# Centring the next image in four batches, one on VectorE and three on GpSimd, with the statistics and the products at other places

## The reference

```
x = x + DCT2(gn(x))                    # gn: per image and channel, (x - mean)/sqrt(var + eps)
y = gn(x)
for k in range(6):                     # Euler steps, dt = 1/6
    h = relu(gn(y)*g1 + b1);  h = conv3x3([t_k, h]) + c1
    h = relu(gn(h)*g2 + b2);  h = conv3x3([t_k, h]) + c2
    y = y + dt*(gn(h)*g3 + b3)
x = x + y
```

## Time and profile before

| | us |
|---|---|
| median of 3 runs | 3807.86 (3799.22 to 3810.55) |
| the profiled execution, its own time | 3808.01 |
| its span in the profile | 3806.2 |
| TensorE busy | 3070.4 (81%) |
| VectorE busy | 2698.6 (71%) |
| ScalarE busy | 2497.2 (66%) |
| GpSimd busy | 1026.3 (27%) |
| mean granted TensorE clock | 0.916 of full speed |

### The profile page before, as it was taken

One profiled execution on the slowest core, in us unless ns is written; L12 is line 12 of the kernel. 1 busy time (PEld: TensorE's weight loads), 2 busy tenths in 40 slices (PEclk: granted clock), 3 DMA queues, 4 the chain that ended last, 5 costly groups with the idle time before them and its releaser, 6 DMA issues.

```text
span 3806.2 us, 147663 instructions
## 1 busy us (share of the span) xinstructions
PE 3070.4 (81%) x61716; PEld 2552.5 (67%) x61716; DVE 2698.6 (71%) x6177; ACT 2497.2 (66%) x3867; POOL 1026.3 (27%) x1405
## 2 busy tenths in 40 slices
PE   3588888888878888788887888888888887888884
PEld 3576767667666666666676766766766666777773
DVE  7577777676767667666776677767776777768783
ACT  0466678566776567756676665866668666687774
POOL 4034312333133331333313333133321334111111
PEclk8799999899999899989998998989999999999997
DMA  3300023112131230312303213032131311321113
GB/s 81 77 20 19 20 53 88 44 53 69 29 88 47 65 69 15 88 54 78 62 3 96 78 45 61 16 91 70 45 61 39 93 45 45 62 69 47 54 45 103
DMA packets 368816, 217.55 MB, mean 57 GB/s; under 512 B 353152, under 2 KB 353520, under 8 KB 366064
## 3 DMA queue, kind: packets, MB, share of 16 engines
q1 hardware_dynamic: 368112, 207.63, 21.4%
HBM read 104.85 MB, written 77.07 MB: 48 GB/s over the span
## 4 chain that ended last, share of the span: by engine, by line
DVE 20%; issue 18%; PE 17%; POOL 17%; ACT 16%; DMA 7%; SPq 3%; DVEq 1%; POOLq 0%; ACTq 0%
POOL xn L556 12%; PE cps L1435 11%; ACT z L659 5%; DMA xs<-in_x_dram 5%; ACT z L689 4%; DVE bnt L1111 3%; PE dps L1543 3%; SPq L438 2%; POOL m L546 2%; DVE hb L1081 2%; DVE y L1085 2%; DVE bn L1130 2%; ACT unread_z L679 2%; DVE ha L1081 1%; DVE bni L1122 1%
## 5 line engine op out<-in xcount | busy, mean ns | idle before, releaser
L1435 PE MATMUL cps<-ha,w 64*64 64x392 f16 (+1 forms) x27648 | 1441.7, 353 | 97.6 <-issue 41.0
L659 ACT ACTIVATE z<-cps,bias_now 128x784 f32<-128x784 f32 (+2 forms) x1056 | 764.2, 740 | 839.1 <-PE cps L1435 833.4
L1435 PE MATMUL cps<-hb,w 64*64 64x392 f16 x27648 | 1274.0, 333 | 33.3 <-POOL hb L523 11.4
L1435 PEld LDWEIGHTS cps<-ha,w 64*64 64x64 f16 x27648 | 1081.8, 112 | 316.8 <-issue 139.3
L1435 PEld LDWEIGHTS cps<-hb,w 64*64 64x64 f16 x27648 | 1075.9, 107 | 134.9 <-issue 47.9
L503 POOL TENSOR_TENSOR small<-small,half 128x1 f32<-128x1 f32 x304 | 168.2, 553 | 1657.3 <-DVE small L1012 1242.1
L1111 DVE BATCH_NORM_STATS2 bnt<-z 128x6 f32<-128x392 f32 (+1 forms) x768 | 388.3, 551 | 238.3 <-ACT z L659 237.8
L1081 DVE TENSOR_TENSOR ha<-z,ha 128x784 f16<-128x784 f32 x384 | 381.4, 993 | 96.0 <-ACT z L689 92.2
L556 POOL TENSOR_SCALAR xn<-xs,m 112x112 f32<-112x112 f32 x448 | 438.6, 993 | 6.0 <-POOL m L551 6.0
L1081 DVE TENSOR_TENSOR hb<-z,hb 128x784 f16<-128x784 f32 x384 | 374.4, 975 | 84.7 <-ACT z L689 77.1
L689 ACT ACTIVATE z<-z,small 128x784 f32<-128x784 f32 x384 | 396.3, 1032 | 0.0
(11 more groups left out here) (161 smaller groups left out, 2679.3 us busy)
## 6 DMA issues: line engine op xcount, KB each, us to landing
xa<-x_dram SPq DMA_DIRECT2D x128, 196.0 KB, 5.0
y<-xa SPq DMA_DIRECT2D x16, 1568.0 KB, 7.5
y_dram<-y SPq DMA_DIRECT2D x128, 196.0 KB, 4.7
xs<-in_x_dram SPq DMA_DIRECT2D x31, 784.0 KB, 8.6
x_dram<-x1s SPq DMA_DIRECT2D x30, 784.0 KB, 5.3
fin<-y_dram SPq DMA_DIRECT2D x30, 784.0 KB, 8.1
fin<-x_dram SPq DMA_DIRECT2D x28, 784.0 KB, 8.5
out_dram<-fin SPq DMA_DIRECT2D x28, 784.0 KB, 3.3
```

The costliest lines, as they stand in the source:

```text
L659: return nc.scalar.activation(dst, src, ACT.Identity, bias=bias_now[parts, conv:conv + 1], **more)
L1435: return pe.matmul(dst, w[hin * 64:(hin + 1) * 64, kx, a, wl, :], src[:, :, 0:NA], start=(what == "X" and n == 0), stop=(what == "Y" and n ...
```

## The change

`normalise_half` is cut in two. `half_bias` (GpSimd) makes the product of mean and scale and stands right behind `half_rsqrt`. The 16 channels become four batches of four: batch 0 is a new `normalise_first` on VectorE, with a semaphore of its own, just ahead of the update of slot 0; batches 1 and 2 stay where all 16 were on GpSimd, batch 3 goes behind slot 1's powers. TensorE waits for each batch alone. On VectorE the statistics of the next half image are spread anew: four channels now stand between `pre_of(Z1, 0)` and `post_of(Z1, 0)`, together with the wait for the arrival of `xs`; then three, three, three, and three inside `post`. `half_post` goes from behind `products_of(1, 2)` to behind `split_for(2, 1)`, `products_of(1, 1)` behind it, and `products_of(1, 3)` ahead of `split_for(2, 3)`. In step FIVE the seven `start_stats` of slot 1 come from the end of FOUR, and `pre_of` and `post_of` of (IZ, 1) come later. On TensorE the statistics products move by some rounds.

```diff
--- before.py
+++ after.py
@@ -260,6 +260,7 @@
         s_xnb = sem("s_xnb")
         s_nb = sem("s_nb")
         xn_done = sem("xn_done")
+        xn_first = sem("xn_first")
         t_done = sem("t_done")
         ts_done = sem("ts_done")
         xp_done = sem("xp_done")
@@ -545,18 +546,21 @@
                 pool.wait_ge(s_m0, NHALF_STEPS * (n + 1))
                 nc.gpsimd.tensor_tensor(m[:, 4, 0:CQ], m[:, 3, CQ:2 * CQ], half[0:H, :], ALU.pow).then_inc(pow0, 1)
 
-            def normalise_half(n):
+            def half_bias(n):
 
                 pool.wait_ge(pow0, n + 1)
                 nc.gpsimd.tensor_tensor(m0[:, 6, CQ:2 * CQ], m0[:, 6, 0:CQ], m0[:, 4, 0:CQ], ALU.mult
                                         ).then_inc(s_nb, 1)
                 pool.wait_ge(s_nb, n - HALVES + 1)
+
+            def normalise(n, b):
+
                 pool.sem_inc(pool_gate, 1)
-                for c in range(CQ):
+                for c in range(4 * b, 4 * b + 4):
                     last = nc.gpsimd.tensor_scalar(xn[:, c, :], xs[:, c, :], m0[:, 4, c:c + 1],
                                                    m0[:, 6, CQ + c:CQ + c + 1], ALU.mult, ALU.add)
                 last.then_inc(xn_done, 1)
-                pool.wait_ge(xn_done, n - HALVES + 1)
+                pool.wait_ge(xn_done, (NBATCH - 1) * (n - HALVES) + b)
 
             def setup():
 
@@ -605,6 +609,7 @@
                 wrap_rows(1, conv_at(g, s, 2), fixes + 1, pows)
                 if kind == MID:
                     half_rsqrt(HALVES * (g + 1) + s, m0)
+                    half_bias(HALVES * (g + 1) + s)
                 if kind == FIVE:
                     rsqrt_of(IY, 0)
                 rsqrt_of(Z2, 0)
@@ -613,11 +618,14 @@
                     return
                 pows = rsqrt_of(*((IY, 1) if kind == FIVE else (Y, 0)))
                 if kind == MID:
-                    normalise_half(HALVES * (g + 1) + s)
+                    normalise(HALVES * (g + 1) + s, 1)
+                    normalise(HALVES * (g + 1) + s, 2)
                 seam(0, conv_at(g, s, 3), fixes + 2, pows)
                 pows = rsqrt_of(Z2, 1)
                 if kind != FIVE:
                     pows = rsqrt_of(Y, 1)
+                if kind == MID:
+                    normalise(HALVES * (g + 1) + s, 3)
                 seam(1, conv_at(g, s, 4), fixes + 3, pows)
                 if kind == FOUR:
                     rsqrt_of(IZ, 0)
@@ -1163,6 +1171,14 @@
                 nc.vector.tensor_scalar(m0[:, 3, CQ:2 * CQ], m0[:, 4, CQ:2 * CQ], 0.0, EPS, ALU.max, ALU.add
                                         ).then_inc(s_m0, 1)
 
+            def normalise_first(n):
+
+                dve.wait_ge(s_nb, n - HALVES + 1)
+                for c in range(4):
+                    last = nc.vector.tensor_scalar(xn[:, c, :], xs[:, c, :], m0[:, 4, c:c + 1],
+                                                   m0[:, 6, CQ + c:CQ + c + 1], ALU.mult, ALU.add)
+                last.then_inc(xn_first, 1)
+
             def half_add(b, n, src, buffers=FIRST):
 
                 dve.wait_ge(xp_done, n + 1)
@@ -1277,52 +1293,58 @@
 
                 dve.wait_ge(bn_done, 1 + 2 * u)
                 pre_of(Z1, 0, 9)
+                if kind == MID:
+                    dve.wait_ge(xs_in, 16 * first_place(hn) + 16)
+                    half_stats(range(0, 4))
                 post_of(Z1, 0)
-                if kind == FIVE:
-                    dve.wait_ge(ibn_done, SLOTS * (g + 1) + 2)
-                    pre_of(IZ, 1, 7)
                 stats_of(0, 0)
                 split_for(1, 0)
                 if kind == MID:
-                    dve.wait_ge(xs_in, 16 * first_place(hn) + 16)
-                    half_stats(range(0, 4))
+                    half_stats(range(4, 7))
                 split_for(1, 1)
                 stats_of(0, 1)
                 if kind == MID:
-                    half_stats(range(4, 8))
+                    half_stats(range(7, 10))
+                if kind == FIVE:
+                    start_stats(1, g + 1, range(7))
+                    dve.wait_ge(ibn_done, SLOTS * (g + 1) + 2)
+                    pre_of(IZ, 1, 7)
                 split_for(1, 2)
+                stats_of(0, 2)
+                stats_of(0, 3)
+
+                dve.wait_ge(bn_done, 2 + 2 * u)
+                pre_of(Z1, 1, 9)
                 if kind == FIVE:
                     post_of(IZ, 1)
-                stats_of(0, 2)
-                stats_of(0, 3)
-
-                dve.wait_ge(bn_done, 2 + 2 * u)
-                pre_of(Z1, 1, 9)
                 split_for(1, 3)
-                post_of(Z1, 1, meanwhile=(lambda: half_stats(range(8, 12))) if kind == MID else None)
                 if kind == MID:
-                    half_stats(range(12, CQ))
+                    half_stats(range(10, 13))
+                post_of(Z1, 1, meanwhile=(lambda: half_stats(range(13, CQ))) if kind == MID else None)
+                if kind == MID:
                     half_pre(hn)
                 dve.wait_ge(y_new[0], 16 * (g + 1))
                 dve.wait_ge(y_new[1], 16 * (g + 1))
                 products_of(1, 0)
                 split_for(2, 0)
                 split_for(2, 1)
-                products_of(1, 1)
+                if kind == MID:
+                    half_post(hn, stats_before(g, s, kind) + STATS[MID].index((X0, 0)))
                 if kind == FIVE:
                     post_of(IY, 0)
                 if kind == FOUR:
                     start_stats(0, g + 1, (0, 1, 2))
+                products_of(1, 1)
                 split_for(2, 2)
                 if kind == FOUR:
                     start_stats(0, g + 1, (3, 4, 5, 6))
                     dve.wait_ge(ibn_done, SLOTS * (g + 1) + 1)
                     pre_of(IZ, 0, 7)
                 products_of(1, 2)
+                products_of(1, 3)
+                split_for(2, 3)
                 if kind == MID:
-                    half_post(hn, stats_before(g, s, kind) + STATS[MID].index((X0, 0)))
-                split_for(2, 3)
-                products_of(1, 3)
+                    normalise_first(hn)
 
                 update(0, lambda: euler(0, 0))
                 euler(0, 1)
@@ -1375,7 +1397,6 @@
                 added(3)
                 if kind == FOUR:
                     post_of(IZ, 0)
-                    start_stats(1, g + 1, range(7))
 
             with dve.Fori(0, GROUPS - 1) as g:
                 for s in range(HALVES):
@@ -1597,22 +1618,23 @@
 
                     pe.wait_ge(x1_done, NBATCH * hn + b + 1)
                     if b == 0:
-                        pe.wait_ge(xn_done, hn - HALVES + 1)
+                        pe.wait_ge(xn_first, hn - HALVES + 1)
+                    else:
+                        pe.wait_ge(xn_done, (NBATCH - 1) * (hn - HALVES) + b)
                     dct_rows(b, NBATCH * hn + b, dps)
 
-                between = {(1, 8): lambda: statistics_of(Z1, 0)}
+                between = {(2, 0): lambda: statistics_of(Z1, 0)}
+                convolve(1, 0, s, 0, conv_at(g, s, 0), sets, between)
+
+                between = {(2, 0): lambda: statistics_of(Z1, 1)}
+                if kind == MID:
+                    between[5, 0] = lambda: half_mean(hn, stats_before(g, s, kind) + STATS[MID].index((X0, 0)))
                 if kind == FIVE:
-                    between[5, 0] = lambda: statistics_of(IZ, 1)
-                convolve(1, 0, s, 0, conv_at(g, s, 0), sets, between)
-
-                between = {(1, 8): lambda: statistics_of(Z1, 1)}
-                if kind == MID:
-                    between[6, 0] = lambda: half_mean(hn, stats_before(g, s, kind) + STATS[MID].index((X0, 0)))
-                if kind == FIVE:
+                    between[1, 0] = lambda: statistics_of(IZ, 1)
                     between[5, 0] = lambda: statistics_of(IY, 0)
                 convolve(0, 1, s, 1, conv_at(g, s, 1), sets + 1, between)
 
-                between = {(1, 8): lambda: statistics_of(Z2, 0)}
+                between = {(1, 10): lambda: statistics_of(Z2, 0)}
                 if kind == FIVE:
                     between[6, 0] = lambda: statistics_of(IY, 1)
                 convolve(1, 1, s, 2, conv_at(g, s, 2), sets + 1, between)
```

More of the change, by code:

```diff
@@ L1291, in step @@
                 if kind == MID:
-                    half_stats(range(4, 8))
+                    half_stats(range(7, 10))
[3 more added lines that the diff above has]
+                    pre_of(IZ, 1, 7)
                 split_for(1, 2)
-                if kind == FIVE:
-                    post_of(IZ, 1)
                 stats_of(0, 2)
@@ L1300, in step @@
                 pre_of(Z1, 1, 9)
+                if kind == FIVE:
+                    post_of(IZ, 1)
                 split_for(1, 3)
-                post_of(Z1, 1, meanwhile=(lambda: half_stats(range(8, 12))) if kind == MID else None)
                 if kind == MID:
-                    half_stats(range(12, CQ))
+                    half_stats(range(10, 13))
```

(2 more changed lines are left out.)

## The result

The changed kernel takes **3634.8 us** (median of 4 runs, 3623.7 to 3640.13) against 3804.75 us for the kernel before on the same chip (4 runs, 3799.22 to 3810.55): a ratio of 0.9549, 95% interval 0.9520 to 0.9579, that is 170 us faster. Forecast was 3681, range 3620 to 3750. The profiled execution took 3623.7 us, the fastest of the four, with a span of 3621.9 and a mean granted clock of 0.936 where it was 0.916; so the two profiles lie 184 us apart and the medians 170.

The account below looks back on a forecast made before the run. No engine was taken to bound the kernel; TensorE's 28 waits for GpSimd's centring, 207.5 us, and the half clock after them were the price. 66 + 28 - 3 + 27 + 6 + 3 = 127; 3808 - 127 = 3681 us, range 3620 to 3750.

Parts of the forecast that it names:

- steps 1 to 3 lose or gain over 3 us: Sign that the forecast is wrong, read in the 21 MID steps that are not step 0 of a group.
- The wait for xs: VectorE, ahead of slot 0's coefficients in steps 1 to 3: 21 waits of about 8.5 us, some 180 us.
- TensorE's new idle: Ahead of conv2 of slot 0 in steps 1 to 3: 5 to 6 us, with the low clock there.
- the rival of the long slow clock: Conv2 of slot 0 runs 9 us at half clock in 21 steps: 59 us more, 3740; chance 0.13.
- GpSimd: Eight channels ahead of the power for slot 1's update cost 0.1 us in each of 28 steps, 3 us lost.
- normalise_first: Its four operations on VectorE ahead of slot 0's update take 0.8 us; by the Trainium skill an estimated 0.5 us.
- Step 0: 66 forecast: First MID step of each of 7 groups: 7.5 us less each, 52.5, plus 13.2 for slow stretches: 66 us gained.
- the four long slow stretches: Half-clock stretches of some 9 us after TensorE's centring wait in four step 0s; their going gains 4 x 3.3 = 13.2 us.
- Steps 1 to 3: 28 forecast: 21 MID steps: 17 us and 30 us gained, 9 and 10.5 lost to later landing and slow clock: 28 us gained.
- the walk: Delay followed through steps 1 to 3: slot 0's update 6.4 us late, slot 1's 0.8 us earlier of a possible 7.5.
- FOUR, FIVE and the last group: 27 + 6 + 3 = 36 forecast: FIVE's moved bn_stats 27 us, its front idle shrinking to some 2.2; FOUR's earlier last product 6; last group 3.
- The rival of a hidden load: The wait for xs delays nothing, so the 21 steps gain 7.5 us each: 3522 us; chance 0.05.

Follow-up runs that it names:

- e5: The changed kernel with batch 0 centred on GpSimd too, so four signalled batches there and none on VectorE: 3699.31 us.
- e1: The changed kernel with the wait for xs and the next half image's statistics back at their old places: 3503.9 us.
- e7: The changed kernel with xs loaded in four pieces of four channels, each as soon as the addition has read its channels: 3479.16 us.
- e4: The kernel before with only the moves of slot 1's statistics in FIVE and at the end of FOUR: 3785.69 us.
- e2: e1 with the moves of slot 1's statistics in FIVE and the end of FOUR undone as well: 3523.64 us.
- e6: The kernel before with only the last product ahead of the last split and the statistics products of Z1 and Z2 some rounds later: 3772.13 us.
- e3: The kernel before with only the wait for xs and the first four statistics moved ahead of slot 0's coefficients: 3914.66 us.

## Why the prediction was right, and where it was off

**Sign, size and mechanism held, with luck in the size.** The time lies in the range, 46 us under the forecast by the median. The forecast named a sign of being wrong, that steps 1 to 3 lose or gain over 3 us, and this sign came: they gain 3.1 us each, 3.5 in groups 1 to 6. So one term was clearly off, and the range was wide enough to hold it. The wait for xs: forecast 21 times about 8.5 us, some 180; measured 192.1 in 22, of which one, 5.1 us, is the first load of the run. TensorE's new idle: forecast 5 to 6 us; measured 5.4 to 7.1 in the 21 steps, with 2.7 to 6.0 us of half clock behind it, 4.3 in the mean, where 4.3 was forecast from one row. It never lasted 9 us, so the rival of the long slow clock fell.

**GpSimd.** Charged 0.1 us a step; the power came 0.44 us after VectorE wanted it instead of 0.33 ahead of the other update: 0.1. The rule of the Trainium skill that spoke against it (GPSIMD Engine Reference, "Key points") is true in kind, and the trace agrees: the second batch took 1.98 us a channel while VectorE split and multiplied, the last batch 0.60. What it does to this kernel showed only in e5.

**normalise_first.** Charged 0.8 us by the four bn_stats; from 279.89 to 280.88 it is 1.0. The Trainium skill's figure (VectorE: DVE Perf Modes, "The TRN2 errata") gave an estimated 0.5; the trace does not agree with it, and the nearest row was the better guide.

**Step 0: 66 forecast, 75 measured.** The update of slot 1 came not 7.5 but 8.2 us earlier, 5 us in seven steps. The other 4 lie behind it: in groups 1 to 6 that part shrinks by 2.9 us, where the four long slow stretches had been taken as 13.2/6 = 2.2. Averages from the trace over groups 1 to 6, us from the start of the step:

| | conv2 of slot 0 | update of slot 0 | update of slot 1 | next step |
|---|---|---|---|---|
| step 0, before | 10.9 | 34.4 | 58.1 | 83.0 |
| step 0, after | 10.0 | 33.8 | 49.9 | 72.0 |
| steps 1 to 3, before | 11.7 | 32.1 | 55.7 | 80.2 |
| steps 1 to 3, after | 17.5 | 38.6 | 54.7 | 76.7 |

**Steps 1 to 3: 28 forecast, 66 measured. This is the term that was mis-sized**, 38 of the 57 us between the forecast and the profiled execution (184 against 127). In group 0 the three steps won 2.5 us, the 0.8 each of the walk. In the 18 others the table shows 5.8 us lost at conv2 and 6.4 at the update of slot 0, as walked through ("6.4 us at the update of slot 0"). Then two steps of the sum failed.
- The forecast gained 0.8 at the update of slot 1 and took off 0.5 for the later landing and 0.5 for the slow stretch. Measured is 1.1 gained. The measured 6.4 us have the later landing and the slow stretch in them, so nothing is left to charge beside them. For the landing the waits show why: in groups 1 to 6 VectorE waits 0.5 us longer for xs than in group 0, 9.0 against 8.5 us, but it did so before the change too, 1.4 against 0.9, and only the difference between the kernels counts. Some 1.3 us a step, 23 us.
- Behind the update of slot 1 the steps have 24.5 us before and 22.0 after, 2.5 less, where the forecast had 30/18 = 1.7 for the long slow stretches. A short one was priced at nothing. TensorE idles 1.9 us ahead of the last DCT product in both kernels, and behind this idle came 3.4 us at half clock in 17 of these 18 steps before, and in 5 of 18 now (the windows above show the four of group 1, of which the first is a step 0). A stretch of 3.4 us costs 1.7: 12 x 1.7 = 20 us, by this estimate, enough for the 14 that are left. That it is the clock, the windows show; why the grant differs behind equal idles was not tried. Over all 24 MID steps of groups 1 to 6 it is 23 before, 8 after, 15 in e1 and 9 in e7.

**FOUR, FIVE and the last group: 27 + 6 + 3 = 36 forecast, 43 measured, by two errors that cancel.** FIVE's moves were taken at 3.8 us a group, 27; alone they give 17.5 in e4's profile and 11.3 between those of e1 and e2, 1.6 to 2.5 a group. The forecast's idle of 2.2 us does not follow from its own rows either: 6.74 less 3.7 is 3.0, and e4, with this move alone, has 3.16. The idle did go, but FIVE itself became 1.1 us longer a group in e4, which the text had at nothing. The last product ahead of the split and the later statistics product were taken at 0.9 a group in FOUR and 0.7 a step in the last; e6 shows 2.3 a group in FOUR, 1.5 in FIVE, which had no term at all, and 8 us in the last group, 1.7 a step. That the two errors cancel is luck. The parts measured alone, 17.5 and 26 in FOUR and FIVE, add up to more than the 36 that the changed kernel has there, so they overlap. The row that I used has one of several such waits; the row of the waits, 97.4 us in 51, would have given the better bound: e6 halves it.

The main reading was right: step 0 pays in full, and steps 1 to 3 lose most of their gain to the load. The rival of a hidden load put their full gain at 157 + 30 = 187 us; e1, with the wait at its old place, has 186, and the changed kernel 66. The step that was argued best, program order on VectorE, is the one that held best: 6.4 us late at the update of slot 0 forecast, 6.6 measured in group 0, where the walk was made, and 6.4 later.

## What to carry to other kernels

A wait on an engine that works in order delays all that is queued behind it, so look what that is before an operation with a transfer as input is moved forward; if it must go forward, first bring its input forward, in pieces that each wait for the last reader of their own part (here 156 us). When a producer signals once at the end and the consumer takes the data in parts, signal each part: with the batches placed by when they are wanted, this was some 200 of the 261 us available in these steps, and signals and places were not tried apart. When a delay is walked through a step, charge each cause once, at the milestone where it is read, and look at the total row of a wait and not at one of its instances.

## What was not expected of the hardware

The granted clock behind equal idles is not the same, and no run shows why. TensorE's idle of 1.85 us in the kernel before and 1.93 in the changed one, ahead of the same product, was followed by 3.4 us at 0.51 in 23 of 24 cases before and in 8 of 24 after. And the idles of 7.3 to 7.7 us before the first DCT product were followed by 3.1 to 3.7 us of half clock in 14 steps, 5.6 in one and 9.4 to 9.8 in 13, while 21 new idles of 5.4 to 7.1 us in another phase were never followed by more than 6.0.

In e3, which keeps the wait for xn and adds the one for xs, only 2 of the 28 idles before that product were followed by over 7 us at half clock.

The pieces of the load, 196 KB each, landed in 2.5 to 6.2 us in e7 (median 4.7), and the whole of 784 KB in 8.0 to 9.6 in the changed kernel (median 8.5), both counted from 240 us on. Cutting it cost SyncE's queue 3.26 us of issue (2.20 and 1.06) instead of 1.05.
